# Scores and maxima over all 128 rows, zero rows behind the stacks, and another order of the squares in the mix stage

## What is computed

```python
x = x + attention(layernorm(x))          # 16 heads of 32 features
x = x + ffn(layernorm(x))

# attention
query = heads(ct_q @ Wu_q_w + b) + heads(rope(ct_q @ Wq_r_w + b))   # ct_q = x @ Wd_q_w + b
key   = heads(ct_kv @ Wu_k_w + b) + heads(rope(x @ Wk_r_w + b))     # ct_kv = x @ Wd_kv_w + b
value = heads(ct_kv @ Wu_v_w + b)
out = softmax(query @ key.T / sqrt(528)) @ value @ Wo_w + Wo_b

# ffn: x_prev is x moved by one token
xr = mu_r * x + (1 - mu_r) * x_prev
xk = mu_k * x + (1 - mu_k) * x_prev
ffn = sigmoid(xr @ W_r.T) * (relu(xk @ W_k.T) ** 2 @ W_v.T)
```

## Time and profile before

| | |
|---|---|
| median of 3 runs | 3019.98 us |
| profiled execution, its own time | 3021.54 us |
| its span, first to last instruction | 3019.8 us |
| PE matmul busy | 2965.3 us, 98% |
| DVE / ACT / POOL busy | 73% / 49% / 67% |
| fold, project, attend, mix end at about | 41, 653, 2256, 3020 us |
| granted TensorE clock, mean | 0.995 |

### The profile page before, as it was taken

The page is one execution under the profiler, slowest core; times in us unless marked ns, Lnnn a source line. Parts: engine busy times, 40 slices in busy tenths (PEclk is TensorE's granted clock), DMA queues, the critical chain, the costliest instruction groups (busy, mean ns, idle before and its releaser), DMA issues. The chain is left out here.

```text
span 3019.8 us, 42725 instructions
## 1 busy us (share of the span) xinstructions
PE 2965.3 (98%) x15424; PEld 2002.6 (66%) x15424; DVE 2198.5 (73%) x3371; ACT 1481.9 (49%) x2716; POOL 2012.0 (67%) x704
## 2 busy tenths in 40 slices
PE   8999999999999999999999999999999999999999
PEld 5888888865555555555555555555547777787777
DVE  5555566597777877777777777777787777677774
ACT  2222222236666666666666666666663323323232
POOL 1111111229999999999999999999953555565553
PEclk9999999999999999999999999999999999999999
DMA  4455555764646464646464646464551332323321
GB/s 151 168 176 175 171 171 178 209 165 103 151 103 151 103 151 102 151 102 151 102 151 102 151 102 151 102 151 103 136 151 48 107 96 71 111 60 107 96 70 42
DMA packets 189081, 380.72 MB, mean 126 GB/s; under 512 B 17376, under 2 KB 53376, under 8 KB 180992
## 3 DMA queue, kind: packets, MB, share of 16 engines
q1 hardware_dynamic: 180000, 313.70, 37.7%
q0 software_dynamic: 8928, 65.02, 10.5%
HBM read 194.59 MB, written 118.49 MB: 104 GB/s over the span
## 5 line engine op out<-in xcount | busy, mean ns | idle before, releaser
L444 DVE TENSOR_REDUCE part_max<-ps_m 128x1 f32<-128x512 f32 x1984 | 1210.9, 684 | 279.4 <-PE ps_m L428 278.7
L1156 POOL TENSOR_TENSOR pairs<-probs 128x2048 f32<-128x2048 f32 x248 | 1153.3, 4661 | 111.1 <-ACT probs L1130 110.9
L1130 ACT ACTIVATE probs<-ps_s 128x512 f32<-128x512 f32 x2012 | 1016.6, 623 | 262.1 <-PE ps_s L1021 245.8
L428 PE MATMUL ps_m<-k_stack,q_stack 96*128 96x512 f32 x1984 | 818.4, 413 | 2.1 <-PEq L476 2.1
L1021 PE MATMUL ps_s<-q_stack,k_stack 97*128 97x512 f32 x2012 | 795.5, 397 | 0.0
L428 PEld LDWEIGHTS ps_m<-k_stack,q_stack 96*128 96x128 f32 x1984 | 376.9, 190 | 238.6 <-DVE part_max L444 104.5
L1034 PE MATMUL ps_o<-probs,v_tiles 128*32 128x512 f32 x4096 | 492.5, 598 | 0.0
L1021 PEld LDWEIGHTS ps_s<-q_stack,k_stack 97*128 97x128 f32 x2012 | 380.7, 189 | 105.6 <-ACT probs L1130 2.8
L1163 POOL TENSOR_TENSOR pairs<-pairs 128x2048 f32<-128x2048 f32 x62 | 284.3, 4585 | 4.9
L691 POOL TENSOR_TENSOR ln_rstd<-ln_rstd,ln_minus_half 128x4 f32<-128x4 f32 x15 | 15.1, 1009 | 403.9 <-DVE ln_rstd L733 403.9
L1034 PEld LDWEIGHTS ps_o<-probs,v_tiles 128*32 128x32 f32 x4096 | 107.0, 109 | 234.3 <-issue 174.9
(11 more groups left out here) (200 smaller groups left out, 4900.6 us busy)
## 6 DMA issues: line engine op xcount, KB each, us to landing
pairs<-pairs POOLq DMA_DIRECT2D x62, 1024.0 KB, 8.0
q_stack<-q_hi_scratch SPq DMA_DIRECT2D x128, 256.0 KB, 5.5
k_stack<-k_hi_scratch SPq DMA_DIRECT2D x64, 512.0 KB, 10.9
x_in<-in_x SPq DMA_DIRECT2D x16, 1024.0 KB, 5.6
q_hi_scratch<-st_hi SPq DMA_DIRECT2D x64, 256.0 KB, 2.3
q_lo_scratch<-st_lo SPq DMA_DIRECT2D x64, 256.0 KB, 2.6
k_hi_scratch<-st_hi SPq DMA_DIRECT2D x64, 256.0 KB, 2.4
k_lo_scratch<-st_lo SPq DMA_DIRECT2D x64, 256.0 KB, 2.7
```

The lines of the kernel that those rows point to most:

```text
L428: nc.tensor.matmul(bank[:, :], att["q"][r][0:ROWS, half, h, q * P:(q + 1) * P], att["k"][r][0:ROWS, h, kc * CH:(kc + 1) * CH], start=True, ...
L444: nc.vector.reduce_max(part_max[:, half, j, kc:kc + 1], bank[:, :], AX).then_inc(att["m_read"], 1)
L1130: nc.scalar.activation(probs[:, (r * UNITS + u) % PR, x // HG, x % HG, :], bank(n, place(u * UT + x))[:, :], ACT.Exp, scale=SCALE).then_in ...
L1156: nc.gpsimd.tensor_tensor(pairs[:, w, :, :], probs[:, (r * UNITS + u) % PR, 0, :, :], probs[:, (r * UNITS + u) % PR, 1, :, :], ALU.add).th ...
```

## The change

1. Maxima and scores contract over all 128 rows (`att["q"][r][:, ...]` and `att["k"][r][:, ...]`, no `0:ROWS`).
2. Rows 97 to 127 hold zeros. In slot 0, two DVE memsets over rows 96 to 127 write them in the fold block. In slots 1 and 2, DMAs fill them once, from one 512-element piece of each zero row of slot 0; the row of ones comes with them, so that the two copies of line 984 and the wait on `rows_set` go.
3. Row 96 of the queries must be zero while the maxima are made. A one-row DMA writes it ahead of each load but slot 0's first.
4. Mix, DVE: `square_lo(0)` stands between the low part of xr and the last row statistics, `square_lo(1)` between the statistics and the normalisation. Mix, POOL: the power stands behind the first two squares.

```diff
+            nc.vector.memset(att["q"][0][ROWS:P, :, :, :].bitcast(F32), 0.0)
+            nc.vector.memset(att["k"][0][ROWS:P, :, :].bitcast(F32), 0.0).then_inc(empty_set, 1)
             nc.vector.memset(bd_cols[:], 1.0).then_inc(ones_set, 1)
...
+            dve.wait_ge(empty_set, 1)
             nc.vector.memset(att["k"][0][ROWS:ROWS + 1, :, :].bitcast(F32), 1.0)
...
+EMPTY_LOADS = 4
+def loaded_count(r, loads):
+    return 16 * (LOADS * loads + (loads - 1) + (EMPTY_LOADS if r > 0 else 0))
...
-    att["q"].append(q[0:ROWS + 1, :, :, :])
-    att["k"].append(k[0:ROWS + 1, :, :, :].rearrange(...))
+    att["q"].append(q[:, :, :, :])
+    att["k"].append(k[:, :, :, :].rearrange(...))
...
 def load_group(sp, att, scratch, n, r):
+    def fill(which, first, last, src):
+        sp.dma_start(rows_of_slot(which, first, last),
+                     src.broadcast_to([last - first, HG * NQ, CH])).then_inc(att["loaded"][r], 16)
+    zeros = att["q"][0][ROWS + 1:P, 0, 0:1, :].bitcast(F32)
+    if n == r and r > 0:
+        fill("q", ROWS + 1, P, zeros)
+        fill("k", ROWS + 1, P, zeros)
+        fill("k", ROWS, ROWS + 1, att["k"][0][ROWS:ROWS + 1, 0:1, 0:CH].bitcast(F32))
+    if n != r or r > 0:
+        fill("q", ROWS, ROWS + 1, zeros[0:1])
     for part, src in enumerate((qh_d, ql_d, qh_d)):
...
-        pe.wait_ge(att["loaded"][r], 16 * LOADS * loads)
+        pe.wait_ge(att["loaded"][r], loaded_count(r, loads))
-    nc.tensor.matmul(bank[:, :], att["q"][r][0:ROWS, half, h, q * P:(q + 1) * P],
-                     att["k"][r][0:ROWS, h, kc * CH:(kc + 1) * CH], ...)
+    nc.tensor.matmul(bank[:, :], att["q"][r][:, half, h, q * P:(q + 1) * P],
+                     att["k"][r][:, h, kc * CH:(kc + 1) * CH], ...)
...
-            for r in range(1, R3):
-                sp.dma_start(ks[r][ROWS:ROWS + 1, :, :].bitcast(F32),
-                             ks[0][ROWS:ROWS + 1, :, :].bitcast(F32)).then_inc(rows_set, 16)
...
-                if u == 0 and x == 0 and type(n) is int and n == 1:
-                    pe.wait_ge(rows_set, 16 * (R3 - 1))
...
-                    if more:
-                        inv_std(c + 1)
                     for g in range(FC):
+                        if g == RELU and more:
+                            inv_std(c + 1)
                         pool.wait_ge(relu_done, c * FC + g + 1)
...
-            def norm(c, par):
+            def norm(c, par, square_lo):
...
                 shift_low_r(c - 1)
+                square_lo(0)
                 for s in range(0 if type(c) is int and c == 1 else TPC - 2, TPC):
                     row_stats(c, par, s)
                 statistics(c)
+                square_lo(1)
                 normalise(c, par)
...
-                        norm(c + 1, 1 - par)
+                        norm(c + 1, 1 - par, square_lo)
...
-                    for g in range(FC):
+                    for g in range(2 if more else 0, FC):
                         square_lo(g)
```

More of the change, by code:

```diff
@@ L88, in fold_block @@
         k_sum = sem("fold_k_sum")
+        empty_set = sem("empty_set")
         ones_set = sem("fold_ones_set")
@@ L321, in group_views @@
     q, k, v = slot
-    att["q"].append(q[0:ROWS + 1, :, :, :])
-    att["k"].append(k[0:ROWS + 1, :, :, :].rearrange("p n f d -> p (n f d)").rearrange("p (a t) -> p a t", a=HG))
+    att["q"].append(q[:, :, :, :])
+    att["k"].append(k[:, :, :, :].rearrange("p n f d -> p (n f d)").rearrange("p (a t) -> p a t", a=HG))
     att["v"].append(v)
@@ L403, in load_group, with rows_of_slot @@
     qh_d, ql_d, kh_d, kl_d, v_d = scratch
+    def rows_of_slot(which, first, last):
+        return att[which][r][first:last].bitcast(F32).rearrange("p a b t -> p (a b) t" if which == "q" else "p a (b t) -> p (a b) t",
+                                                                **({} if which == "q" else {"b": NQ}))
+    def fill(which, first, last, src):
[8 more added lines that the diff above has]
+        fill("q", ROWS, ROWS + 1, zeros[0:1])
     for part, src in enumerate((qh_d, ql_d, qh_d)):
@@ L425, in max_product @@
     if u == 0:
-        pe.wait_ge(att["loaded"][r], 16 * LOADS * loads)
+        pe.wait_ge(att["loaded"][r], loaded_count(r, loads))
     h, q = divmod(j, QT)
-    nc.tensor.matmul(bank[:, :], att["q"][r][0:ROWS, half, h, q * P:(q + 1) * P],
-                     att["k"][r][0:ROWS, h, kc * CH:(kc + 1) * CH], start=True, stop=True).then_inc(att["m_scored"], 1)
+    nc.tensor.matmul(bank[:, :], att["q"][r][:, half, h, q * P:(q + 1) * P],
+                     att["k"][r][:, h, kc * CH:(kc + 1) * CH], start=True, stop=True).then_inc(att["m_scored"], 1)
 def max_reduce(nc, dve, att, banks, m, u):
@@ L896, in bank @@
             return ps_s[v % SR] if w is None else wide[w % WR]
-        rows_set = sem("rows_set")
         scored = sem("scored")
```

## The result

| | before | after |
|---|---|---|
| median, 4 runs each | 3019.99 us (3019.28 to 3020.96) | 3045.36 us (3044.73 to 3046.41) |
| ratio, 95% interval | | 1.0084 (1.0067 to 1.0102) |
| span of the profiled execution | 3019.8 us | 3043.3 us |
| mean granted clock | 0.995 | 0.987 |
| first scores of group 0 start at | 653.42 us | 690.56 us |

The change costs 25 us: 37.1 us in the last project chunk, 23.4 in group 0 and 1.3 in group 1 are lost; 9.2 in the steady groups and 29.1 at the end come back. The start of group 0 moves by itself: in the kernels without 31-row or spread fills ahead of the last project chunk's stores it lies between 651.8 and 653.9 us, so a loss in front of it is known to about 1.5 us.

A forecast was written before the change was run, and what follows sets the result against it. It took PE as never idle for long in attend, with ACT ending units, and PE waiting for relu in mix. 3021.54 - 25.5 - 6 + 35.8 + 17 = 3042.8, less 1.6 for the median: 3041 us, range 3010 to 3078.

The forecast's parts named there:

- mix: Mix block: PE's wait for the third relu goes in 15 chunks; -25.5 us, bounds 0 and -26.
- full rows: Attend block: matmul steps shorten over 128 rows, but ACT ends most units; -6 us, bounds 0 and -38.
- slot 1's fills: Last project chunk: fills delay loads and stores, so ACT waits at item 4, then DVE and PE; +35.8 us.
- slot 2's fills: Start of group 0: fills, loads and POOL's transfers make group 1's first maxima wait 15.1 us; +17 us with slow clock.
- One engine for 31 rows: DMA fills: each 31-row fill runs on one engine as 248 packets of 2 KB, 21.8 us a fill.
- rival "spread": DMA fills run on many engines and cost only 4 to 5 us of queue; 2988 us, chance 0.16.
- The first engine's share of the loads: SP's queue after slot 1's fills: 229 KB on the first engine, 9.2 or 16 us; 10 taken.
- The hole: Mix block, each chunk: the gate product stops ahead of its third tile for the key product's third relu; 1.64 us lost.
- rival 2: Attend block: full rows bring the whole 38 us because ACT's pace falls with the matmuls'; 3009 us, chance 0.05.
- rivals of slow service: DMA fills: one engine, served as slowly as in the loads; 3109 us, chance 0.05 between 3080 and that.
- a hole that comes back in each chunk of the mix block: Mix block: the hole returns at another wait, xk's low part or POOL's power; 3066 us, chance 0.05.

The follow-up runs named there:

- spread fills: Changed kernel, same zeros in cuts of 16 and 32 rows instead of 31-row fills: 2987.13 us, ratio 0.9886.
- ACT relieved: Exponential over 320 of 512 columns from group 1: 2981.28 us against 128 rows with zeros cut by 16 and 32; 2990.83 us against mix order alone.

## Why the prediction was right, term by term

The forecast of 3041 us missed by 4.4 us, with the right sign. The terms, against what the traces show:

| term | forecast, us | measured, us |
|---|---|---|
| mix | -25.5 | -28.5 (alone, in medians) |
| full rows | -6 | -9.2 (29 groups x 0.317) |
| slot 1's fills | +35.8 | +37.1 |
| slot 2's fills | +17 | +24.7 (23.4 in group 0, 1.3 in group 1) |
| sum | +21.3 | +24.1 |

With the 29.1 us that the trace has from group 31 to the end in place of the 28.5, the sum is 23.5 us, the difference of the spans; the medians differ by 25.4. The small miss is luck in part: the gains came out 6.2 us larger than forecast and the cost of the fills 9.0 us larger.

- **One engine for 31 rows: right**, the step that decided. A packet took 0.081 us against 0.088. The rival "spread" gave 2988 us; the spread cut measured 2987.1. It is the right number for a kernel other than this one. But its number is right by errors that cancel: it held that item 4 could bear the fills, where PE lost 4 to 6 us, and it took 31.5 us for the mix order and the rows, which brought about 38.
- **The first engine's share of the loads: the term that this mis-sized.** The prediction took 10 us for it, "since that engine is then alone", and named 16 us, at the rate of the loads, as the other value. That rate was the better one. SP stood in its issue (12.09 and 21.42 us), so no load left before 629.97, and the other fifteen engines ran their shares not 30 us ahead of the first one's, as the prediction had it, but at the same time. From the fills' end at about 637 to the last load's landing at 654.0 are 17 us. That the engines slow each other there is the reading of the rates (190 to 224 GB/s, 12 to 14 an engine, against 25 for the first one alone); no run separates it. At slot 1, fills that ended about 4 us earlier than forecast (0.081 us a packet against 0.088) hid half of that: item 4 was released at 655.38 against 652.1. PE stood for 36.0 us against the 33.8 of the forecast, and lost 2.8 us to the slow clock against 2.0. Of these 38.8 us the table shows 37.1, as the block before started late within its spread, at 653.42.
- **Slot 2** is where it shows, 24.7 against 17. The forecast had 43.6 us of fills, 10 of loads and 9.1 of POOL's accumulating transfers, 62.7 in sum. In the trace SP sends the loads 42.3 us after the block's start (732.90 less 690.56), and group 1's maxima start 28 us later, at 761: 70.4 in sum. In these 28 us the engines move 175 GB/s, under the 225 of the earlier trace rows. POOL's second transfer of the group is among them, and how much of the 28 us is its own isn't separated by any run.
- **Mix: right, 10% short.** The hole goes in all 15 chunks. The prediction read 1.64 us at the hole; a chunk gave 1.85, since small waits at other products went as well.
- **Full rows: 3 us short, and the reason wrong.** I took 0.2 us a group, since ACT would end nearly every unit, and 38 us as the bound if it did not. The groups gave 0.32. ACT was not what held them: over 96 and 97 rows, relieving it brings 0.06 us a group. With ACT relieved the rows bring 13 us, so the bound, which is rival 2's too, was wrong: it used the step of the mix block (0.2267 us), which the first four of a unit's 14 steps do not reach in any run here. And what costs is not that rows are missing but that their number changes from one matmul to the next.
- By the rule of the Trainium skill (TensorE: Matmul & The Clock Gate, section LDWEIGHTS) that rows don't matter for a weight load, the rows term was to be 0. The weight loads themselves agree (0.19 us for 97 and for 128 rows); the groups do not stay, they lose 0.32 us. With equal row counts the groups agree with it too: 97 rows cost what 128 cost.

The rivals of slow service and of a hole that comes back in each chunk of the mix block did not happen; single late chunks, as shown above, are in some executions of later kernels and not in this one.

## What to carry to other kernels

Before you add a transfer, look at how its first dimension divides: 31 rows ran on one of sixteen engines, 32 rows on all, and the difference was 58 us in this kernel. Then look at the queue it stands in and who waits at its end; in a pause of the queue the same bytes, well cut, cost nothing beyond the spread of the start (653.89 us against 651.8 to 653.9). And try the cheapest form of an idea: equal row counts gave all of the gain that full rows gave, with no zeros to bring.

## What the runs showed that was not expected

- **SP can be held in its issue by a transfer on one engine.** While one engine works off 31-row fills, the issue of the next takes 12 us and of the one after 21 to 29 us, against 0.4 to 0.5 us for a load before; with 17 rows in place of 31 the longest of SP's rows for two fills is 13.75 us. Then transfers that could run on fifteen idle engines are not even sent. What limits the queue (packets, transfers, or something else) was not tried.
- **Matmuls whose row count alternates between 96 and 97 take 233 ns a step at a unit's end, and over 128 rows throughout 227 ns**, when ACT does not hold them. Over 97 throughout this was measured only at ACT's full pace, with a mean step of 233.4 ns against 233.7 over 128 and 237.1 over 96 and 97. Whether 96 against 97 is special, or any change of count costs this, was not tried. The Trainium skill (TensorE: Matmul & The Clock Gate, section on the array as 16 x 32x32) says the array consists of sixteen sub-arrays of 32 x 32, and that a tile's position in it works in strips of 32. By that, 97 and 128 rows take four strips and 96 rows three; no run here separates the strips from the count.
- **A wait that is removed takes small ones with it**: 0.2 us a chunk beyond the hole itself.
